# Moving operands of the second mixture's products addressed by TensorE registers that are loaded from a table

## The reference, cut to what matters

```python
def _L1_ffn_ref(x, gate_w, gate_b, w1, b1, w2, b2, w3, b3, ws1, bs1, ws2, bs2, ws3, bs3):
    # 16 experts of 176 hidden features, top 6; a shared expert of 352; xf is 2048 x 256
    probs = softmax(xf @ gate_w.T); idx = top_k(probs + gate_b, 6); cw = probs at idx, else 0
    for each expert:
        h = silu(xf @ W1.T + B1) * (xf @ W3.T + B3)
        y = y + c[:, None] * (h @ W2.T + B2)
    z = silu(xf @ ws1.T + bs1) * (xf @ ws3.T + bs3) @ ws2.T + bs2
    return y + z
```

## Time and profile before

| | us |
|---|---|
| median of 2 runs | 2143.03 |
| the runs | 2140.89 and 2145.17 |
| span of the profiled execution | 2139.0 |
| TensorE busy in it | 2077.7 |

### The profile page before, as it was taken

The page is one execution under the profiler, slowest core; times in us unless marked ns, Lnnn a source line. Parts: engine busy times, 40 slices in busy tenths (PEclk is TensorE's granted clock), DMA queues, the critical chain, the costliest instruction groups (busy, mean ns, idle before and its releaser), DMA issues. The chain is left out here.

```text
span 2139.0 us, 33422 instructions
## 1 busy us (share of the span) xinstructions
PE 2077.7 (97%) x12193; PEld 1588.5 (74%) x12193; DVE 1455.7 (68%) x2761; ACT 1221.1 (57%) x2435; POOL 576.8 (27%) x679
## 2 busy tenths in 40 slices
PE   8999999999999999989999999999999999999997
PEld 6888888888788888877777765333334688778886
DVE  5666666677667666666656567999994557655555
ACT  5666666666556666554444335888887434444433
POOL 3444444444334444332221110000000112222221
PEclk9999999999999999999999999999999999999999
DMA  2000000000000000011111202100000111111111
GB/s 75 20 21 18 16 21 21 21 21 21 9 21 21 21 21 20 4 38 45 38 44 40 56 22 44 24 19 22 21 12 1 43 37 45 45 45 45 45 52 57
DMA packets 55143, 64.67 MB, mean 30 GB/s; under 512 B 10268, under 2 KB 35655, under 8 KB 54983
## 3 DMA queue, kind: packets, MB, share of 16 engines
q1 hardware_dynamic: 54982, 62.55, 10.5%
HBM read 52.42 MB, written 2.10 MB: 25 GB/s over the span
## 5 line engine op out<-in xcount | busy, mean ns | idle before, releaser
L868 POOL TENSOR_TENSOR a_pr<-a_pr,a_rinv 128x512 f32<-128x512 f32 (+3 forms) x384 | 312.2, 827 | 474.7 <-DVE a_rinv L1118 474.7
L86 PE MATMUL psum<-xh,g_hi_gu 128*128 128x512 f32 x920 | 375.5, 408 | 7.8 <-DVE f_hid L1612 6.3
L88 PE MATMUL psum<-xh,g_lo_gu 128*128 128x512 f32 x920 | 359.8, 391 | 0.0
L87 PE MATMUL psum<-xl,g_hi_gu 128*128 128x512 f32 x920 | 359.2, 390 | 0.0
L1208 POOL TENSOR_TENSOR g_lo_gu<-g_raw_gu,g_hi_gu 128x512 fp32r<-128x512 f32 x84 | 108.8, 1295 | 758.5 <-ACT g_hi_gu L1204 758.5
L1926 ACT ACTIVATE a_pt<-psum 128x512 f32<-128x512 f32 x512 | 276.2, 597 | 59.2 <-PE psum L1826 37.9
L1945 DVE TENSOR_REDUCE x_m_negm<-psum 128x1 f32<-128x1024 f32 x240 | 290.8, 1224 | 13.5 <-PE psum L1811 11.2
L1546 ACT ACTIVATE f_act_s<-psum,g_gu_bias 128x512 f32<-128x512 f32 (+1 forms) x168 | 115.1, 685 | 295.5 <-PE psum L88 295.3
L1625 DVE TENSOR_TENSOR f_hl<-f_hid,f_hh 128x512 fp32r<-128x512 f32 x164 | 115.6, 705 | 226.3 <-ACT f_hh L1558 224.6
L1023 ACT ACTIVATE a_pr<-psum,a_negm 128x128 f32<-128x128 f32 (+7 forms) x256 | 190.1, 742 | 107.0 <-DVE a_negm L1108 102.9
L1030 ACT ACTIVATE a_pth<-psum 128x512 fp32r<-128x512 f32 (+3 forms) x384 | 174.7, 489 | 113.1 <-PE psum L927 107.7
(11 more groups left out here) (316 smaller groups left out, 4302.3 us busy)
## 6 DMA issues: line engine op xcount, KB each, us to landing
g_raw_gu<-in_gu SPq DMA_DIRECT2D x82, 256.0 KB, 2.8
f_raw_dn<-in_down SPq DMA_DIRECT2D x82, 128.0 KB, 2.0
g_raw_gu<-in_qkv SPq DMA_DIRECT2D x32, 256.0 KB, 2.8
a_wvr<-in_qkv SPq DMA_DIRECT2D x32, 128.0 KB, 2.4
a_wor<-in_o SPq DMA_DIRECT2D x32, 128.0 KB, 2.0
x_queries_qq<-x_qhi SPq DMA_DIRECT2D x128, 32.0 KB, 1.9
yT<-in_xT SPq DMA_DIRECT2D x4, 512.0 KB, 6.6
x_queries_qq<-x_qlo SPq DMA_DIRECT2D x64, 32.0 KB, 1.9
```

What stands on the lines that cost most here:

```text
L86: pe.matmul(out, a_hi, b_hi, start=first, stop=False)
L87: pe.matmul(out, a_hi, b_lo, start=False, stop=False)
L88: return pe.matmul(out, a_lo, b_hi, start=False, stop=last)
L868: pool.tensor_tensor(x, x, rinv[:, j:j + 1].to_broadcast([P, count * P]), ALU.mult).then_inc(p_done, 1)
```

## The change

GpSimd fills a table of 2 x 50 words in one partition at the start of the stage: row 0 holds the half of the batch for each K (0 or 1), row 1 the slot K % 2. Every five tiles TensorE loads ten words of it into registers, one `value_load` each with the bounds 0 and 1, and the moving operands of gate, up and down take their place from these registers in place of constants. The values are the same as before, and so are products, order and waits. The weights, `begin_y`, `bias_y` and the side tasks keep constant addresses; so does the first mixture (`biased` is false there).

```diff
+        by_register = biased
+        if by_register:
+            places = ph.sb("places", [1, 2, 2 * NT], mybir.dt.int32)
+            places_set = ph.sem("places_set")
...
+        READ = 5
...
         @block.gpsimd
         def _(pool):
+            if by_register:
+                for half in range(2):
+                    pool.memset(places[:, 0, half * NT:(half + 1) * NT], half).then_inc(places_set, 1)
+                slots = places[:, 1, :].rearrange("p (k s) -> p k s", s=2)
+                for slot in range(2):
+                    pool.memset(slots[:, :, slot], slot).then_inc(places_set, 1)
             if not ready:
                 gu.remainder(pool, 0)
...
         @block.tensor
         def _(pe):
+            half_of, slot_of = {}, {}
+
+            def read_places(K):
+
+                if K == 0:
+                    pe.wait_ge(places_set, 4)
+                for k in range(K, min(K + READ, 2 * NT)):
+                    half_of[k] = pe.value_load(places[0:1, 0, k:k + 1], min_val=0, max_val=1)
+                    slot_of[k] = pe.value_load(places[0:1, 1, k:k + 1], min_val=0, max_val=1)
+
+            def inputs(x, dt, K, c):
+                if not by_register:
+                    return x[:, dt, tokens(K, c)]
+                halves = x[:, dt, :].rearrange("p (b s) -> p b s", b=B)
+                return halves[:, bass.ds(half_of[K], 1), c * CH:(c + 1) * CH].rearrange("p b s -> p (b s)")
+
+            def hidden(h, K, c):
+                if not by_register:
+                    return h[:, K % 2, c, :]
+                return h[:, bass.ds(slot_of[K], 1), c, :].rearrange("p s n -> p (s n)")
...
-                            xh[:, dt, tokens(K, c)], xl[:, dt, tokens(K, c)], dt == 0, dt == DT - 1)
+                            inputs(xh, dt, K, c), inputs(xl, dt, K, c), dt == 0, dt == DT - 1)
...
-                            hh[:, K % 2, c, :], hl[:, K % 2, c, :], False, K % NT == NT - 1)
+                            hidden(hh, K, c), hidden(hl, K, c), False, K % NT == NT - 1)
...
             for K in range(2 * NT + 1):
+                if by_register and K % READ == 0:
+                    read_places(K)
                 for c in range(NC):
                     if K <= LAST:
                         gate(K, c)
```

## The result

The changed kernel takes 2197.55 us (median of 2 runs, 2192.07 and 2203.03) against 2143.03: ratio 1.0257, interval 1.0191 to 1.0324. The profiled execution has a span of 2201.2 us, 62.2 more than before.

What follows compares the result with a forecast made beforehand. TensorE, busy 97% of the span, was taken to bound the kernel. Later batches 10.8 us, first batch 1.7 and waits 0.5 sum to 13 us on 2143.0: 2156 us, range 2142 to 2200.

Steps and rivals of the forecast that it cites:

- the mechanism: Ahead of gate at the ten batches, reads outlast TensorE's queued work and stand bare; 13 us in all, chance 0.57.
- The cover: Work queued for TensorE ahead of gate at tile 40: 3.8 us, of which 3.1 us remain after addressed matmuls and addresses.
- addresses, table, wait, the other engines: In the second mixture, table, wait and 12 addresses a tile at 51 ns stay hidden; other engines don't become late.
- the second rival: At each addressed matmul, TensorE's sequencer becomes the bound, five steps of 51 ns a pair; 2233 us, chance 0.13.
- 0.4 us a word: Price of one checked register load ahead of gate: 0.3 us load plus two 51 ns steps; 4.0 us a batch.
- two steps of 51 ns for the two bounds: In each word's read, the bounds check takes two sequencer steps, 51 ns each, beside a 0.3 us load.
- the 10.8 of the sum: Nine later batches, before tiles 5 to 45, each 1.2 us bare ahead of gate: 10.8 us.
- batches longer than 6 us: wrong in the price of a word: Sign in the profile: batches of reads over 6 us would show that the price of a word was wrong.
- the first batch: Reads before gate of tile 0 start no earlier than the logits at 1671.34; about 1.7 us bare.
- I add nothing for the clock: New TensorE pauses are as short as today's 1.6 us, which left the clock at 1.00; 0 us added.
- all hidden: Rival at the batches: a checked word under 0.28 us, only the first batch shows; 2143 to 2147 us, chance 0.25.
- two slow rivals: Sequencer bound at addressed matmuls, 2233 us, chance 0.13; words priced like small transfers, 1.9 us each, 2305, chance 0.03.

Runs made afterwards that it cites:

- e2: The changed kernel with the same 100 words read two ahead of every tile instead of ten ahead of every fifth; 2150.13 us, ratio 0.9985.
- e7: The changed kernel with eight words read every four tiles, thirteen batches, instead of ten every five; ratio 1.0129 to the kernel before.
- e1: The changed kernel run again without any edit, for its own interval and a second profile; 2189.75 us, ratio 1.0182 to the kernel before.
- e9: The changed kernel with each batch's ten words read by one load and without bounds checks; ratio 0.9992 to the kernel before.
- e4: The changed kernel with each batch split, five words ahead of chunk 0 and five ahead of chunk 1 of every fifth tile; 2155.36 us, ratio 1.0007.
- e8: The changed kernel with each batch's ten words side by side and read by one load, bounds checks kept; 2164.27 us, ratio 1.0062.
- e3: The changed kernel with its reads kept but constant addresses in gate, up and down; 2193.11 us, ratio 1.0205 to the kernel before.
- e10: The changed kernel with its later ten-word batches moved behind gate of chunk 0 of tiles 4, 9 and so on; ratio 1.0308 to the kernel before.
- e6: The changed kernel with twenty words read every ten tiles, five batches, instead of ten every five; ratio 1.0296 to the kernel before.

## Why the prediction was right, and where it was wrong

**Right: the mechanism. Lucky: the number.** The time lies above the one before and, at 2197.55, just inside the upper end of the range. That is owed to the range's width: 13 us more were likeliest, 54.5 were measured, four times as much, and of the two runs one, 2203.03, lies outside. The cost is the part of each batch that the queue doesn't cover, at ten places and nowhere else, named by `issue` on gate's L86, as foretold. The cover was taken as 3.8 us at tile 40 and 3.1 after what the addresses use; measured are 3.6 to 3.7 us over the batches of eight, ten and twenty words with the addresses in the way.

**Right: addresses, table, wait, the other engines.** 12 addresses a tile were forecast and there are 12 (600 in 50 tiles), at 46 and 32 ns against 51. The array's pace within a group is 0.23 us as before, and e2 puts 1800 addressed matmuls at no more than 1.3 us. With that the second rival (2233 us) falls; in e2's stretch around tile 40 TensorE is busy for 48.00 of 48 us.

**Mis-sized: "0.4 us a word".** Its load was right, 0.298 us against 0.3. Its check was not: "two steps of 51 ns for the two bounds" are a 146 ns instruction, an 18 ns one and the time between, 0.29 us together. 0.65 in place of 0.4 makes the batch 6.5 us in place of 4.0. With the cover as foretold all of the 2.5 us would stand bare, 3.7 us in place of 1.2; the cover was 0.6 longer and the time behind the last word 0.1 shorter, so 3.0 were measured, nine times, 16 us more than the 10.8 of the sum. I had taken the one sequencer instruction that the trace showed as the price of any. The test "batches longer than 6 us: wrong in the price of a word" is the one that came true.

**Mis-sized: the first batch**, 1.7 us foretold, 5.5 measured. (The sum there is 0.2 off: 1671.3 + 4.0 + 0.3 is 1.5 us behind 1674.11.) Of the difference, 2.5 us is the word again. The rest is that I let the loads begin with the logits; they began at 1689.0, 1.2 us behind the first logit matmul at 1687.79, because the twelve matmuls and their weight loads stand ahead of them in the stream. That order was in the text of the kernel, and I had used it for tile 40 but not for tile 0.

**Failed: "I add nothing for the clock".** The step was that the new pauses are as short as today's 1.6 us. At 1.2 us they would have been, and e7 bears the condition out: none of its eleven later pauses, up to 1.9 us, was followed by half clock. Behind longer ones it does fall, though not each time: behind six of the ten pauses in the changed kernel's trace and four of the ten in e1's, the first among them in both. The clock costs 12.5 us in the one and 7.4 in the other, about a quarter and a fifth of the mixture's loss. The Trainium skill, "TensorE: Matmul & The Clock Gate", Part 1, says that the array runs at half its clock when TensorE has lately been idle, and at full clock when it has been busy. The trace agrees in kind, 0.43 us between starts behind the pause at tile 35 and 0.23 from 2057.40 on; it doesn't let one say which 3 us pause will do it.

**The rival "all hidden"** had its point at 0.28 us a word with the check. At 0.65 it falls for this kernel, and it is what e2 and e9 do and e4 nearly does. The Trainium skill, "Runtime: NRT & Kernel Launch", Instruction fetch mechanics, has some 200 ns for a register loaded from HBM; from this table in SBUF the trace has 298 ns for a word loaded alone and 108 for each of ten loaded together (e8), so one figure for both doesn't fit here.

**The chances.** 0.83 was given to within 2%. The first measurement is 2.57% with its interval's lower end at 1.91%, and e1 is 1.82% with an upper end of 2.15%: neither can be told from 2%. The change stands at the bound, beyond which my own text put only its two slow rivals, 0.16. That was wrong by its own terms: a word of 0.71 us or more gives ten times (7.1 - 3.1 + 0.3) = 43 us, over 2% with no clock at all, and 0.9 us gives 62 us, 2205, which the range to 2200 doesn't take in though the text says that it does. At the measured 0.65 the same terms give 38 us, 1.8%, and there it is the clock left at nothing that hides how near the bound is.

## What to carry to other kernels

Register reads of TensorE are paid by its sequencer, one after another, and are free as long as a group of them is shorter than the work already queued: on this TensorE some 3.6 us, five checked words (e4), or ten in one load without checks (e9). So spread them (two a tile cost nothing) or load words that lie side by side at once and leave out a bounds check that the program can prove; don't gather single loads into a batch, which saves nothing: 0.65 us a word is the slope from eight words to twenty, and two at a time (e2) are hidden. When a forecast has a pause in it, price the pause with both ends of the unknown duration, and ask at the long end whether the clock falls. And when one profile shows a loss in a stage that wasn't changed, run the same program again before explaining it.

## What the hardware showed that I had not expected

- The bounds check of a loaded word takes 0.29 us (146 ns, 18 ns, and the time between), about as much as the load itself, 0.298.
- A load of ten words side by side takes 1.08 us: dearer than one word, far cheaper than ten.
- Half clock grew much faster than the pauses: 3.4 us for eleven pauses of up to 1.9 us and a longer first (e7), 17, 27 and 31 for ten of about 3 us (e1, after, e3), 65 for ten of about 4 us (e10), 58 for five of about 9 us (e6, 34 of them inside the pauses). Not every 3 us pause is followed by half clock: in the changed kernel those that end at 1754.80 (3.05 us idle), 2099.77 (2.96) and 2143.65 (2.80) weren't, those at 1958.34 (2.87) and 2054.36 (2.88) were, and so was a shorter one, at 1858.86 (2.42). What decides it stays open; none of the runs was made to tell it. Behind the 3.05 us and behind the 2.42:

```profile
1754.80:1760.00 5.20, 5.20 (x23) 4.32 (x24) 2.24 (x3) 2.22 (x4) 1.22 (x1) 1.00 0.00 0
1859.40:1862.70 3.30, 3.30 (x9) 2.53 (x9) 0.00 (x0) 1.20 (x3) 0.00 (x0) 0.50 0.00 0
```

- The clock was at half for 23 us on end in the attention while TensorE was busy 23.00 of 23 us (row 1334 above), with no pause of over 0.4 us in the stage ahead of it; in e1 the same program had 3.4 us of it. Its cause is open too.
